# A windowed-attention and ternary-FFN layer: all masks of the scores in their second pass, one transfer that copies the high query rows, values projected sooner

## The chip, the cores and the metric

The kernel runs on one core of one Trainium2 chip. The time is device microseconds (us) of one execution. All times, in the text and in the rows, are microseconds unless ns is written. Engines are named as in the profile: PE is TensorE (PEld its weight loads), DVE is VectorE, ACT is ScalarE, POOL is GpSimd, SP is SyncE, which here only issues DMAs (SPq in the rows). PSUM is the memory that matmuls write, in eight banks.

## What is computed

The reference, cut to its core. `x` is 4 x 2048 x 256 in float32, 16 heads of 16 numbers, a causal window of 64 positions.

```python
def attn(x):                       # x already layer-normed
    q, k, v = (heads(x @ W.T) for W in (Wq, Wk, Wv))
    bias = where((j <= i) & (j > i - 64), 0.0, -inf)
    p = softmax(q @ k.T / sqrt(16) + bias)
    return merge(p @ v) @ Wo.T

def ffn(x):                        # x already layer-normed
    t = lambda W: clip(round(W / (mean(abs(W)) + 1e-5)), -1, 1)
    return relu(x @ t(W1).T + b1) @ t(W2).T + b2

x = x + attn(layernorm(x))
x = x + ffn(layernorm(x))
```

## The kernel before

**Chunks, slots, positions.** The 8192 tokens are cut into 16 chunks of 512. The program of every engine is one loop over slots n; slot n computes block n of the attention scores, 16 blocks to a chunk, so chunk c has its scores in slots 16c to 16c+15. Around the scores every engine does, in a slot, what a table of numbers at the top of the file puts there. A number in it is a slot, counted so that "position p" in this text is the slot with n mod 16 = p. Stage A of a chunk (layer norm, transposes, projections of keys K, queries Q and values V) runs one chunk ahead of its scores. Stage C (output projection `wo`, second layer norm, transposes `t`, first FFN layer `f`, second FFN layer `y`, in two halves h of 256 tokens) runs one chunk behind. So in the steady part of the program each slot mixes work of three chunks. Engines run ahead of each other as far as semaphores let them.

**Numbers are split in two.** Float32 values are carried as a high and a low float16 part. PE writes a bank, ACT copies the high part out (`c_f`, `c_t`, `a_q`, `a_k`, `a_v` on ACT), then DVE subtracts and writes the low part (same names on DVE). The bank is free when DVE is done.

**Scores of a slot** (`scores`, four head groups g, four slots each). For each of four 32-query blocks there are two matmuls of 96 columns: the first pass (m = 0) multiplies the queries in `qbd` with the keys in `ks`, the second (m = 1) adds the low part of the keys. `qbd[t]` holds high query rows on even partitions and low query rows on odd ones; t = 0 serves the groups 0 and 1, t = 1 the groups 2 and 3. In the groups 0 and 1, from chunk 1 on, the second pass reads `qm` and `kw` instead: these have the high query rows and the low keys on the even partitions and constant mask rows on the odd ones, so that the pass also adds the causal mask. In the groups 2 and 3 a matmul of its own (L1104, 256 columns) writes the mask first. The first slot of each group in each batch element (chunks 0, 4, 8, 12) has another mask matmul (L1100, 384 columns).

**After the scores**: `biggest` (DVE L827, negated maxima `negm`), `exps` (ACT L626), `turn` (DVE L844, transposes to `pt`), `low` (POOL L501 and L503, to `th` and `tl`), `values` (PE L1134, 32 or 36 matmuls, in every fourth slot: positions 0, 4, 8, 12), `o_copy` (ACT L672) and `o_add` (DVE L904). The scores of slot n wait for the exponentials of slot n-3. ACT does the exponentials of slot n-1 in slot n, DVE turns slot n-2 and POOL splits slot n-3.

**Placement.** SP copies the projected parts to their places by DMA: `place_v` (L353, 16 DMAs a chunk), `place_q` (L325, 8 DMAs for t = 1, 12 for t = 0 because the high rows go to `qm` too), `place_k` (L299 for t = 1, L302 and L305 for t = 0). SP takes them in the order of its slots and blocks on the first wait that isn't met.

**Banks.** Stages A and C share the banks 4 to 7 in turn (`_turns`): whoever comes next takes the bank that was taken four uses before, and waits until DVE has emptied it. In the steady part the first y matmul at position 2 (L1234, half 0) takes the bank of `f02`, the third quarter of the first FFN layer of half 0, which PE computes at position 0 and DVE empties at position 1 (L955).

**Where V stands**: `A_V` is (10, 13). PE projects the two halves of V (L1186, 12 matmuls of 256 columns each) at the positions 10 and 13, and DVE writes their low parts (L896) at 11 and 14.

**Start-up on POOL**: `mask_queries` fills `qm` with the mask rows at slot -16 (L397), `mask_keys` fills `kw[0]` and `kw[1]` at the slots 7 and 12 (L403), `clear_values` clears the value tiles (L414).

## Time and profile before

| | |
|---|---|
| three runs, median | 672.59 us (672.04 to 673.84) |
| profiled execution, its own time | 674.08 us |
| span of its trace | 672.3 us |
| PE busy | 645.8 us (96%), 8049 matmuls |
| DVE busy | 610.4 us (91%) |
| ACT busy | 564.0 us (84%) |
| POOL busy | 562.0 us (84%) |
| 16 DMA engines, SP's queue | 155816 packets, 41.27 MB, 29.7% |

The profiled execution is 1.5 us over the median, and 1.8 us longer than its span. Busy shares are means over stages with different limits: the first 100 us (weights, thresholds, first chunks) are not like the rest. Matmuls overlap: a matmul of 256 columns shows 273 ns in the groups, but 16 in a row take 1.75 us in the chain, 0.109 us each. The chain's starts are about 0.16 us later than the timeline's, since it goes by ends.

### The profile page before, as it was taken

Reading aid. Unit: us, or ns where it says so; the run is one execution under the profiler, and the core shown is the slowest. Engines: PE = TensorE matmul, PEld = TensorE weight load, DVE = VectorE, ACT = ScalarE, POOL = GpSimd, SP = SyncE. Lnnn points to the kernel's source line nnn. Section 1 sums busy time; section 2 is a strip of 40 time slices with the busy share of each in tenths; the row PEclk is TensorE's granted clock in tenths of the full one; section 3 lists DMA queues with packets and bytes.
Section 4 is the critical chain, followed back from the end, with each engine's and each line's share of the span. In section 5 each row is a group of like instructions: output and inputs, shape, how many; then the busy total and the mean of one; then the engine's idle time right before and its main releaser. Section 6 shows DMA issues by size and latency. Waiting matters only on the chain.

```text
span 672.3 us, 23905 instructions
## 1 busy us (share of the span) xinstructions
PE 645.8 (96%) x8049; PEld 556.4 (83%) x8049; DVE 610.4 (91%) x1388; ACT 564.0 (84%) x2483; POOL 562.0 (84%) x837
## 2 busy tenths in 40 slices
PE   7677999999999999999999999999999999998997
PEld 5465778889888888988888898888888898887886
DVE  8889799998999999998999999899999989898974
ACT  6787889888989989888998988899898989788722
POOL 8888899888889888888988888888988888798821
PEclk9899899999999999999999999999999999999999
DMA  9453444445344545444454544534454353444110
GB/s 313 104 120 73 113 87 105 98 106 123 73 130 88 134 100 117 106 96 118 83 133 97 131 106 94 127 77 119 98 135 100 65 136 67 103 87 98 37 48 32
DMA packets 187009, 70.19 MB, mean 104 GB/s; under 512 B 155268, under 2 KB 178438, under 8 KB 186888
## 3 DMA queue, kind: packets, MB, share of 16 engines
q1 hardware_dynamic: 155816, 41.27, 29.7%
q10 hardware_dynamic: 31072, 27.40, 13.4%
q8 instruction: 65, 1.06, 0.7%
q14 instruction: 56, 0.46, 0.2%
HBM read 20.35 MB, written 9.44 MB: 44 GB/s over the span
## 4 chain that ended last, share of the span: by engine, by line
PE 84%; DVE 7%; SPq 2%; ACT 2%; issue 2%; DMA 1%; ACTq 1%; DVEq 0%
PE ps L1239 16%; PE ps L1227 15%; PE ps L1134 12%; PE ps L1112 11%; PE ps L1173 11%; PE ps L1200 6%; PE ps L1186 5%; PE ps L1212 2%; PE ps L1104 2%; PE ps L1160 2%; DVE negm L827 2%; ACT p L626 1%; PE ps L1234 1%; SPq L353 1%; DVE pt L844 1%
## 5 line engine op out<-in xcount | busy, mean ns | idle before, releaser
L626 ACT ACTIVATE p<-ps,negm 128x96 f32<-128x96 f32 x1024 | 335.3, 356 | 13.6 <-DVE negm L827 12.8
L503 POOL TENSOR_TENSOR tl<-pt,th 128x384 f16<-128x384 f32 x256 | 235.0, 918 | 20.7
L626 ACT ACTIVATION_READ_ACCUMULATOR p<-ps,negm 128x1 f32 x1024 | 229.2, 224 | 0.0
L827 DVE TENSOR_REDUCE negm<-ps 128x4 f32<-128x384 f32 x256 | 137.8, 538 | 31.3 <-PE ps L1112 28.3
L501 POOL CAST th<-pt 128x384 f16<-128x384 f32 x256 | 128.8, 503 | 28.1 <-DVE pt L844 27.6
L844 DVE STREAM_TRANSPOSE pt<-p 128x384 f32<-128x384 f32 x256 | 143.6, 561 | 2.4 <-ACT p L626 2.2
L1112 PE MATMUL ps<-k,qbd 128*128 128x96 f16 x1536 | 124.8, 207 | 0.0
L1112 PEld LDWEIGHTS ps<-k,qbd 128*128 128x128 f16 x1536 | 112.4, 113 | 9.7 <-issue 0.3
L1134 PE MATMUL ps<-th,vb 128*128 128x96 f16 (+1 forms) x1120 | 99.5, 204 | 1.6 <-DVE osum L904 1.6
L1134 PE MATMUL ps<-tl,vb 128*128 128x96 f16 (+1 forms) x1120 | 99.5, 204 | 0.0
L1227 PE MATMUL ps<-xTCh,w1T 128*128 128x256 f16 x512 | 97.6, 272 | 0.0
L1134 PEld LDWEIGHTS ps<-th,vb 128*128 128x128 f16 x1120 | 95.7, 115 | 1.7 <-issue 1.7
L1134 PEld LDWEIGHTS ps<-tl,vb 128*128 128x128 f16 x1120 | 95.0, 115 | 0.0
L681 ACT ACTIVATE hTh<-ps 128x512 f16<-128x512 f32 x128 | 78.4, 614 | 14.1 <-PE ps L1227 13.6
L955 DVE SCALAR_TENSOR_TENSOR hTl<-ps,hTh 128x512 f16<-128x512 f32 x128 | 86.6, 679 | 1.7 <-ACT hTh L681 1.5
L1227 PE MATMUL ps<-xTCl,w1T 128*128 128x256 f16 x256 | 69.8, 273 | 1.0 <-DVE xTCl L948 1.0
L1227 PE MATMUL ps<-xTCl,w1L 128*128 128x256 f16 x256 | 69.8, 273 | 0.0
L1239 PE MATMUL ps<-w2T,hTl 128*128 128x256 f16 x512 | 66.7, 273 | 0.2 <-DVE hTl L955 0.2
L1239 PE MATMUL ps<-w2T,hTh 128*128 128x256 f16 x512 | 66.7, 273 | 0.0
L1112 PE MATMUL ps<-kw,qm 128*128 128x96 f16 x480 | 56.1, 208 | 0.0
L1239 PEld LDWEIGHTS ps<-w2T,hTl 128*128 128x128 f16 x512 | 49.9, 98 | 6.4 <-DVE hTl L955 0.7
L1239 PEld LDWEIGHTS ps<-w2T,hTh 128*128 128x128 f16 x512 | 49.9, 98 | 5.8 <-ACT hTh L681 0.7
(150 smaller groups left out, 1407.4 us busy)
## 6 DMA issues: line engine op xcount, KB each, us to landing
k<-kst SPq DMA_DIRECT2D x32, 288.0 KB, 3.7
rwide<-parked ACTq DMA_DIRECT2D x32, 256.0 KB
out<-x ACTq DMA_DIRECT2D x32, 256.0 KB, 2.2
qbd<-qs SPq DMA_DIRECT2D x252, 32.0 KB, 2.5
vb<-vd SPq DMA_DIRECT2D x248, 32.0 KB, 2.0
x<-in_L_attn_hidden ACTq DMA_DIRECT2D x15, 512.0 KB, 4.0
kw<-kst SPq DMA_DIRECT2D x30, 192.0 KB, 3.9
k<-kst SPq DMA_DIRECT2D x32, 144.0 KB, 3.3
```

The costliest lines, as they stand in the source:

```text
L501: e.tensor_copy(th[g % 2][:, o], pt[n % 3][:, :]).then_inc(s_hp, 1)
L503: e.tensor_tensor(tl[g % 2][:, o], pt[n % 3][:, :], th[g % 2][:, o], ALU.subtract).then_inc(s_lo, 1)
L626: ins = e.activation(p[:, 96 * u:96 * u + 96], bank[:, 96 * u:96 * u + 96], ACT.Exp, bias=m[:, u:u + 1], accum_out=r[:, u:u + 1])
L681: e.activation(hT[0][:, 2 * f:2 * f + 2, :].rearrange("p a b -> p (a b)"), c_bank(c, f"f{h}{f}")[:, :], ACT.Relu).then_inc(s_chi, 1)
L827: e.tensor_reduce(negm[n % 4][:, :], sbank[n % 3][:, 0:384].rearrange("p (a b) -> p a b", b=96), AX.X, ALU.max, negate=True).then_inc(s_mx, 1)
L844: e.transpose(pt[n % 3][:, :], pr[n % NP][:, :]).then_inc(s_tr, 1)
L955: e.scalar_tensor_tensor(out=lo, in0=c_bank(c, f"f{h}{f}")[:, :], scalar=0.0, in1=hi, op0=ALU.max, op1=ALU.subtract).then_inc(s_cdv, 1)
L1112: ins = e.matmul(bank[:, 96 * u:96 * u + 96], to[:, g % 2, blk % 4, :, blk // 4], keys, start=(g < 2 and c > 0 and not first and m == 0 an ...
L1134: ins = e.matmul(pvbank[:, 32 * i0:32 * i1], lhs, rhs, start=(k == k0 and tt is th), stop=(k == 15), skip_group_check=True)
L1173: ins = e.matmul(bank[:, :], wT[n][wp][:, k, 128 * t:128 * t + 128], xTA[xp][:, k, :], start=(m == 0), stop=(m == 5))
L1227: ins = e.matmul(bank[:, o], w, xTC[xp][:, k, :], start=(xp + k == 0), stop=(xp + k == 2))
L1239: ins = e.matmul(bank[:, o], hT[hp][:, f, t * 128:(t + 1) * 128], w2T[:, f, :], start=False, stop=(f == 7 and hp == 1))
```

## The change

1. `qm` becomes two tiles and `kw` four, and `ks[g]` holds the high keys only. In all four groups the second pass reads `qm` and `kw` from chunk 1 on, with the masks in it. The matmul L1104 stays in chunk 0 only; L1100 stays as it was.
2. `place_q` writes `qbd` only: 8 DMAs for each t. A new step `copy_q` copies the even partitions of `qbd[t]`, 64 rows of 8 KB, to `qm[t]` in one DMA. It waits for the four high DMAs of `place_q`, which have a semaphore of their own now. The scores wait for it too.
3. `place_k` issues L302-like and L305-like DMAs for all four groups: 8 a chunk instead of 6.
4. POOL fills two `qm` tiles (slots -1 and 11) and four `kw` tiles (slots 5, 8, 11, 15). The query mask is loaded to `oT[1]` instead of `pr[0]`, so the first exponentials have no wait on it any more.
5. V is projected at the positions 7 and 9. Numbers move elsewhere too: K of t = 1 from 14 to 13, `wo` from 8 and 11 to 9 and 10, the last y from 9 and 10 to 10 and 11, DMAs of K, Q, V, out and x, `O_SPLIT` from 15 to 14, `R_WIDEN` from 11 to 12, the norm's reciprocal roots from 4 to 6, and start-up slots of chunks 0 and 1.

```diff
-V_LATE = 9
-A_T, A_K, A_Q, A_V = (1, 2), (5, 14), (6, 15), (10, 13)
-A_STATS, A_RSTD, A_NORM = (-24, -14), -12, (-7, -6)
+V_LATE = (8, 11)
+A_T, A_K, A_Q, A_V = (1, 2), (5, 13), (6, 15), (7, 9)
+A_STATS, A_RSTD, A_NORM = (-24, -14), -10, (-6, -5)
...
-W_WO, K_MASK = (-6, -2), (7, 12)
-V_CLEAR = (8, 15, 19, 22, 26)
+W_WO, K_MASK, Q_MASK = (-7, -2), (5, 8, 11, 15), (-1, 11)
+V_CLEAR = (10, 15, 19, 21, 26)
...
+        def copy_q(e, c, t):
+            e.wait_ge(d_q[t], 64 * (c + 1))
+            if c == 1:
+                e.wait_ge(s_zm, t + 1)
+            to, src = (z[t][:, :, :, :, :].tensor for z in (qm, qbd))
+            e.dma_start(bass.AP(tensor=to, offset=0, ap=[[2 * 4096, 64], [1, 4096]]),
+                        bass.AP(tensor=src, offset=0, ap=[[2 * 4096, 64], [1, 4096]])).then_inc(d_qm[t], 16)
...
+                if c:
+                    e.wait_ge(d_qm[g // 2], 16 * c)
+                e.wait_ge(d_k[g], 32 * (c + 1))
                 if first:
                     e.matmul(bank[:, 0:384], identb[:, :], maskf[:, :], start=True, stop=False, skip_group_check=True)
-                elif g >= 2 or c == 0:
+                elif c == 0:
...
-                        to = qm if g < 2 and m and c else qbd[g // 2]
-                        keys = (ks[g][:, m, 32 * blk:32 * blk + 96] if g >= 2 or not m else kw[g][:, blk, :] if c
+                        to = qm[g // 2] if m and c else qbd[g // 2]
+                        keys = (ks[g][:, 32 * blk:32 * blk + 96] if not m else kw[g][:, blk, :] if c
```

How the order moves, at three places of the steady part. First DVE, from `o_add` (its first row) at position 13 on, before: the low part of the second V half is `vd`.

```order
L904 TENSOR_TENSOR osum<-ps,ohalf 64x512
L827 TENSOR_REDUCE negm<-ps 128x4
L948 TENSOR_TENSOR xTCl<-ps,xTCh 128x512
L844 STREAM_TRANSPOSE pt<-p 128x384
L827 TENSOR_REDUCE negm<-ps 128x4
L896 SCALAR_TENSOR_TENSOR vd<-ps,vd 128x2x256
L926 BN_STATS stC<-x 128x6 x2
```

DVE at the same place in the changed kernel; `kst` is the low part of the keys.

```order
L901 TENSOR_TENSOR osum<-ps,ohalf 64x512
L824 TENSOR_REDUCE negm<-ps 128x4
L945 TENSOR_TENSOR xTCl<-ps,xTCh 128x512
L841 STREAM_TRANSPOSE pt<-p 128x384
L824 TENSOR_REDUCE negm<-ps 128x4
L886 SCALAR_TENSOR_TENSOR kst<-ps,kst 128x512
L923 BN_STATS stC<-x 128x6 x2
```

The V part has left this place, and the key part has come forward by one slot; behind it the two orders are the same up to the first y.

PE from the transposes `t` of position 12 to the first matmuls of position 14, before.

```order
L1212 MATMUL ps<-identf,xnC 128x128 x4
L1104 MATMUL ps<-maskf,identb 128x4x2x32
L1112 MATMUL ps<-k,qbd 128x96 x8
L1186 MATMUL ps<-wvh,xTAh 128x256 x2
L1186 MATMUL ps<-wvl,xTAh 128x256 x2
L1186 MATMUL ps<-wvh,xTAl 128x256 x2
L1186 MATMUL ps<-wvh,xTAh 128x256 x2
L1186 MATMUL ps<-wvl,xTAh 128x256 x2
L1186 MATMUL ps<-wvh,xTAl 128x256 x2
L1104 MATMUL ps<-maskf,identb 128x4x2x32
```

PE there in the changed kernel.

```order
L1212 MATMUL ps<-identf,xnC 128x128 x4
L1112 MATMUL ps<-k,qbd 128x96
L1112 MATMUL ps<-kw,qm 128x96
...
L1173 MATMUL ps<-xTAh,wkh 128x512 x2
L1173 MATMUL ps<-xTAh,wkl 128x512 x2
L1173 MATMUL ps<-xTAl,wkh 128x512 x2
```

The two mask matmuls and the twelve V matmuls have left; the six K matmuls stand at position 13 instead of 14.

SP's DMAs over one chunk, before.

```order
L353 DMA vb<-vd 32x8x64 x16
L325 DMA qbd<-qs 16x8x128 x8
L299 DMA k<-kst 128x1x1152 x2
L325 DMA qbd<-qs 16x8x128 x4
L325 DMA qm<-qs 16x8x128 x4
L325 DMA qbd<-qs 16x8x128 x4
L302 DMA k<-kst 128x1x576
L305 DMA kw<-kst 64x16x96
```

SP's DMAs in the changed kernel, from V on.

```order
L347 DMA vb<-vd 32x8x64 x16
L299 DMA k<-kst 128x1x576
L301 DMA kw<-kst 64x16x96
L299 DMA k<-kst 128x1x576
L301 DMA kw<-kst 64x16x96
L316 DMA qbd<-qs 16x8x128 x8
L326 DMA qm<-qbd 64x4096
```

Keys of t = 1 now go ahead of the queries of t = 1, and the copy to `qm` is behind both. For t = 0 keys, queries and copy now all stand ahead of V.

## Rows read from the trace of the kernel before

**Rows 1.** Page, part 1: busy us (share of the span) and instructions, the line of all engines.
```profile
PE 645.8 (96%) x8049; PEld 556.4 (83%) x8049; DVE 610.4 (91%) x1388; ACT 564.0 (84%) x2483; POOL 562.0 (84%) x837
```
**Rows 2.** Windows: us, busy of PE, PEld, DVE, ACT, POOL (instructions), PE clock, DMA, GB/s.
```profile
25.00:50.00 25.00, 17.99 (x214) 14.26 (x212) 22.48 (x51) 21.13 (x104) 22.42 (x33) 0.86 0.48 110
75.00:100.00 25.00, 22.45 (x305) 18.72 (x303) 22.96 (x54) 22.77 (x107) 23.27 (x35) 1.00 0.40 92
425.00:450.00 25.00, 25.00 (x340) 22.31 (x338) 23.45 (x56) 22.14 (x102) 21.96 (x35) 1.00 0.41 91
```
**Rows 3.** Chain of work around one chunk: start, us, engine, line and count.
```profile
416.22 1.45 PE ps L1134 x36
...
436.12 1.44 PE ps L1134 x36
...
438.04 0.11 PE ps L1104
...
438.49 1.31 PE ps L1186 x12
...
450.12 0.12 PE ps L1234
...
454.96 1.45 PE ps L1134 x36
```
**Rows 4.** Groups of PE's instructions by line: busy us, mean ns, idle before.
```profile
L1104 PE MATMUL ps<-maskf,identb 128*128 128x256 bf16 x126 | 34.6, 275 | 3.7 <-DMA k<-kst 2.0 <-ACT p L626 1.7
```
**Rows 5.** Timeline of ACT, DVE and PE between the values of position 12 and y.
```profile
437.60 0.59 ACT L672 ACTIVATE ohalf<-ps 64x512 f32<-64x512 f32 x1 [0.48 <-PE ps L1134]
438.22 0.69 DVE L904 TENSOR_TENSOR osum<-ps,ohalf 64x512 f32<-64x512 f32 x1
440.95 0.67 DVE L896 SCALAR_TENSOR_TENSOR vd<-ps,vd 128x512 f16<-128x512 f32 x1
441.55 0.73 DVE L926 BATCH_NORM_STATS2 stC<-x 128x6 f32<-128x256 f32 x2
449.22 0.68 DVE L955 SCALAR_TENSOR_TENSOR hTl<-ps,hTh 128x512 f16<-128x512 f32 x1
449.96 0.28 PE L1234 MATMUL ps<-bp,ones 128*128 128x256 f16 x1
```
**Rows 6.** Timeline of PE, first y of the last chunk's slots, where stage A is absent.
```profile
605.47 0.82 PE L1239 MATMUL ps<-w2T,hTl 128*128 128x256 f16 x6
606.45 0.39 PE L1239 MATMUL ps<-w2T,hTl 128*128 128x256 f16 x2 [0.17 <-DVE hTl L955]
```
**Rows 7.** Timeline of SP and PE, last chunk: DMA issues, and scores that wait for keys.
```profile
613.83 1.22 SPq L299 DMA_DIRECT2D k<-kst  x2
617.35 0.27 PE L1104 MATMUL ps<-maskf,identb 128*128 128x256 bf16 x1 [2.02 <-DMA k<-kst]
```
**Rows 8.** Timeline of SP in one chunk: start and length of issues.
```profile
441.66 11.47 SPq L353 DMA_DIRECT2D vb<-vd  x16
414.48 5.90 SPq L325 DMA_DIRECT2D qbd<-qs  x8
434.84 1.42 SPq L305 DMA_DIRECT2D kw<-kst  x1
```
**Rows 9.** DMA issues: KB each, median us from issue to landing.
```profile
k<-kst SPq DMA_DIRECT2D x32, 288.0 KB, 3.7
x<-in_L_attn_hidden ACTq DMA_DIRECT2D x15, 512.0 KB, 4.0
kw<-kst SPq DMA_DIRECT2D x30, 192.0 KB, 3.9
```
**Rows 10.** Timeline of POOL in the start-up: start, us, idle before in brackets.
```profile
8.43 1.90 POOL L397 COPY qm<-p 128x2048 f32<-128x2048 f32 x1 [0.95 <-DVE xnA L850]
35.11 1.47 POOL L403 COPY kw<-oTl 128x1536 f16<-128x1536 f16 x1
72.15 0.96 POOL L414 MEMSET vb<- 128x1024 f32 x1 [2.05 <-DVE w2T L820]
```

More of the change, by code:

```diff
@@ L65, in v_at @@
     c = stage_a(n, A_V[t])
-    return c if t else 1 if n == V_LATE else None if c == 1 else c
+    return 0 if n == F_V[t] - 16 else c if c and c > 1 else 1 if n == V_LATE[t] else None
 def spread(n, pos, soonest):
@@ L131, in _turns @@
     late = {("C", NCH - 1, "wo1"): E_WO[1] + 0.5, ("C", NCH - 1, "t1"): E_T[1] - 0.5}
-    order = [(V_LATE if (stage, c, name) == ("A", 1, 4) else 16 * (c + (1 if stage == "C" else -1)) + late.get((stage, c, name), p), stage == "A", i, stage, c, name)
+    order = [(V_LATE[name - 4] if (stage, c) == ("A", 1) and name in (4, 5) else F_V[name - 4] - 16 if (stage, c) == ("A", 0) and name in (4, 5) else 16 * (c + (1 if stage == "C" else -1)) + late.get((stage, c, name), p), stage == "A", i, stage, c, name)
              for c in range(NCH) for i, ((stage, name), p) in enumerate(pos.items())]
@@ L200, in build @@
         qbd = [sb(f"qbd{t}", [128, 2, 4, 128, 4], f16) for t in range(2)]
-        qm = sb("qm", [128, 2, 4, 128, 4], f16)
-        ks = [sb(f"k{g}", [128, 1 + g // 2, 64 + CH], f16) for g in range(4)]
-        kw = [sb(f"kw{g}", [128, 16, 96], f16) for g in range(2)]
+        qm = [sb(f"qm{t}", [128, 2, 4, 128, 4], f16) for t in range(2)]
+        ks = [sb(f"k{g}", [128, 64 + CH], f16) for g in range(4)]
+        kw = [sb(f"kw{g}", [128, 16, 96], f16) for g in range(4)]
         vd = sb("vd", [128, 4, 2, 4, 16, 4], f16)
@@ L232, in build @@
         d_w = {n: sem(f"d_w{n}") for n in "qkvo12"}
-        d_q = [sem(f"d_q{t}") for t in range(2)]
+        d_q, d_ql, d_qm = ([sem(f"{n}{t}") for t in range(2)] for n in ("d_q", "d_ql", "d_qm"))
         d_k = [sem(f"d_k{g}") for g in range(4)]
@@ L265, in build @@
         n1, n2 = n1.rearrange("p (a b) -> p a b", b=256), n2.rearrange("p (a b) -> p a b", b=1024)
-        smask, kmask = pr[0][:, 0:256].bitcast(f16), oT[1][:, 1, 0:96]
+        smask, kmask = oT[1][:, 0, :], oT[1][:, 1, 0:96]
         bt = (hT[0][:, :, :].rearrange("p a b -> p (a b)").bitcast(f32), hT[1][:, 0:2, :].rearrange("p a b -> p (a b)").bitcast(f32))
         below = hT[1][:, 4:8, :].rearrange("p a b -> p (a b)").bitcast(f32)
-        first_kl = [kw[g][:, :, :].rearrange("p a b -> p (a b)")[:, 0:64 + CH] for g in range(2)]
+        first_kl = [kw[g][:, :, :].rearrange("p a b -> p (a b)")[:, 0:64 + CH] for g in range(4)]
         def by_four(bank):
@@ L293, in place_k @@
                     e.wait_ge(s_sc, 16 * (c - 1) + 4 * g + 4)
-                if c == 1 and t == 0:
+                if c == 1:
                     e.wait_ge(s_kw, g + 1)
@@ L376, in _ @@
                     if c is not None:
-                        place_q(e, c, t, (0, 1, 2) if c or t else (0,))
+                        place_q(e, c, t, (0, 1) if c or t else (0,))
                         if c + t == 0:
                             place_k(e, 0, 0, (1,))
+                    c = stage_a(n, Q_COPY[t])
+                    if c is not None and c >= 1:
+                        copy_q(e, c, t)
                 c = spread(n, V_DMA, 17)
@@ L527, in _ @@
                     mask_keys(K_MASK.index(n))
+                if n in Q_MASK:
+                    mask_queries(Q_MASK.index(n))
                 for h in range(2):
@@ L705, in _ @@
                 if n == A_Q[0] + 2 - 16:
-                    place_q(e, 0, 0, (2,))
+                    place_q(e, 0, 0, (1,))
                 if n in X_LATE:
@@ L1108, in scores @@
                     for m in range(2):
-                        to = qm if g < 2 and m and c else qbd[g // 2]
-                        keys = (ks[g][:, m, 32 * blk:32 * blk + 96] if g >= 2 or not m else kw[g][:, blk, :] if c
+                        to = qm[g // 2] if m and c else qbd[g // 2]
+                        keys = (ks[g][:, 32 * blk:32 * blk + 96] if not m else kw[g][:, blk, :] if c
                                 else first_kl[g][:, 32 * blk:32 * blk + 96])
                         ins = e.matmul(bank[:, 96 * u:96 * u + 96], to[:, g % 2, blk % 4, :, blk // 4], keys,
-                                       start=(g < 2 and c > 0 and not first and m == 0 and u == 0),
+                                       start=(c > 0 and not first and m == 0 and u == 0),
                                        stop=(m == 1 and u == 3), skip_group_check=True)
```

69 lines of the change are left out of this document (28 added, 41 removed).

## The prediction, made before the changed kernel ran

> **What bounds the kernel now.** I read the shares first: PE is busy for 96% of the span, DVE for 91%, ACT and POOL for 84% [rows 1]. A mean doesn't tell which stage is bound by what, so the windows come next: in a window of the steady part PE is busy for 25.00 of 25.00 us, DVE for 23.45 [rows 2]. In the start-up PE is busy for 17.99 us between 25 and 50 and for 22.45 us between 75 and 100 [rows 2], so others set the pace there. From about 92 to 600 us PE is the bound, without a gap. A chunk takes 454.96 - 416.22 = 38.74 us [rows 3]; DVE's share of that is 23.45 / 25 x 38.74 = 36.3 us. So a chunk can lose at most 2.4 us before DVE is full, and DVE must have no gap anywhere for that.
>
> **The masks go.** L1104 runs 126 times [rows 4]; 12 are in chunk 0 and stay, 114 go, 8 in each later chunk less 6 for the first slots of the chunks 4, 8 and 12, which have the other mask. The groups show 275 ns for one, which is its latency; the chain gives 0.11 us from one to the next [rows 3], and the y matmuls of the same 256 columns 0.109. So 114 x 0.109 = 12.4 us of PE work. 8 of them stand in chunk 1, in a stretch in which PE has gaps anyway [rows 2], so I count 106 x 0.109 = **11.6 us**. The second pass costs PE the same with either operand.
>
> **What V's move does to DVE.** This is the step on which the prediction rests. Between the values of position 12 and the y of position 2 DVE has hardly a gap: values end, ACT copies their half at 437.60, DVE adds at 438.22, and from there on DVE works through to the low part of `f02`, which starts at 449.22 and takes 0.68, so ends at 449.90. PE starts y at 449.96 [rows 5], in the bank that this very instruction empties. So PE has 0.06 us to spare there, in a kernel that seems to be bound by PE alone. From the last value to y PE takes 450.12 - 437.56 = 12.56 us by the chain (437.56 is 436.12 + 1.44) [rows 3]. The other way, ACT's copy, DVE's work and two hand-overs, takes about 12.5.
>
> The change shortens the two by different amounts. PE loses the 12 V matmuls, 1.31 us [rows 3], and the mask matmuls of the positions 13, 14 and 15, 0.33: it needs 12.56 - 1.64 = 10.92 us. DVE loses only the low part of V, 441.55 - 440.95 = 0.60 us [rows 5]: about 11.85. K of t = 1 moves inside the stretch and changes neither sum. So PE comes to y 0.93 us early and waits for the bank: **a new stall of 0.9 us in every chunk**, where 0.87 us of masks is saved. Both kernels have y's of half 0 in 14 chunks before the scores end: 14 x 0.9 = 12.6 us.
>
> Could DVE be faster in this stretch? Its anchor is the addition of the values (`o_add`), and that can't start before PE has written them; what DVE does earlier (one V part less at position 11, one at 8 and one at 10 more) is over by then, since there PE's slots keep V's 1.31 us. Position 12 itself gets shorter on PE and DVE alike. Bounds of the stall: 0.4 if DVE had 0.5 us of hidden waits inside (the profile shows under 0.1), 1.3 if ACT's or POOL's part of the chain slips by 0.4: POOL's second norm of the half 1 tiles comes after both multiplications and splits, since `O_SPLIT` moved up. 0.9 stands since each term has its row.
>
> The trace holds a trial of this. In the last chunk's slots stage A is absent, so PE lacks 0.44 us of transposes ahead of y while DVE's part of this is the same. There the last two low matmuls of y start at 606.45, though six of 0.109 from 605.47 end at 606.12 [rows 6]: PE stands for 0.33 us, for DVE. 0.44 us taken from PE gave back 0.11.
>
> **The last chunk's keys.** At the scores of slot 248 PE waits 2.02 us for the keys of t = 1, which SP issues last, at 613.83 [rows 7]. In the changed kernel V is issued some 5 us sooner and the keys stand right behind it; last is the copy to `qm`. V's 16 DMAs take 11.5 us, four of keys at most 1.4 each, 8 of queries 5.9 [rows 8], the copy 0.6 and a landing like that of 512 KB, 4.0 [rows 9]. Counted from the V part at position 10, that is 2.4 + 11.5 + 3.4 + 5.9 + 0.6 + 4.0 = 27.8 us; in the steady part the scores of group 2 come 34 us after it, in the last chunk, with its short slots, about 29. So the wait goes: **-2.0 us** (bounds -2.0 and 0).
>
> **DMA traffic.** Per chunk two copies of 512 KB and two more `kw` placements of 192 KB come, four query DMAs go. A copy is priced between a 288 KB placement, 3.7, and the 512 KB load, 4.0 [rows 9]; to 8 us if an 8 KB row doesn't spread. All of it is hidden by the 6 us above, and by over 10 us for t = 0, which is ahead of V. The `kw` placement moves 192 KB in pieces of 192 B in 3.9 us, the keys' 288 KB in 3.7 [rows 9]: 1.6 times longer per byte.
> The Trainium skill ("DMA: Bandwidth & Descriptors", Specifications) asks for pieces of at least 512 B for full rate, which speaks against two more such placements. The trace agrees as to the rate; by that rule too the sum stays while the cover holds, and it is the third rival if it doesn't.
>
> **Start-up.** POOL gets two mask copies of 1.47 us and one of 1.90 more [rows 10] between 28 and 60 us; the first of 1.90 moves from 8.43 to the time before the first split, and V's early projection lets POOL place it 1 us sooner, which covers half. POOL has 25 - 22.42 = 2.6 us of gaps between 25 and 50 [rows 2], and DVE's turns have three tiles of lead, so I expect nothing there. Later, the clearing at slot 22 already waits 2.05 us for a weight [rows 10]; at slot 21 it waits for the same weight with one split fewer done, so POOL is 1.4 us later at about 73 us and works without a gap until 100. By then DVE, not POOL, leads most of the time: **+0.5 us** (bounds -1 and +4.5).
>
> **Sum.** -11.6 + 12.6 - 2.0 + 0.5 = -0.5 us. Against the profiled execution's 674.08 that is 673.6; it lies 1.5 over the median, so 672.59 - 0.5 = **672.1 us**. The masks' time is given back at y.
>
> **Rivals.**
> - *The cover holds.* If y doesn't wait, since DVE's work has more give than I read (its instruction starts are 0.44 to 0.60 us apart, no one is proven tight), all of the masks count: 672.6 - 11.6 - 2.0 + 0.5 = 659.5. For it: 25 of 25 us of PE, DVE at 94% only. Against it: the 0.06 us and the stall in the last chunk. Half a stall gives 665.8. Chance 0.22.
> - *Slower: POOL in the start-up.* The 4.8 us of mask copies and the 1.4 us at the clearing put POOL behind by more than the lead of three `pt` tiles. DVE's turn of a slot waits for POOL's split of three slots before; once POOL is later than that lead, about 4 us, DVE stops, with it the exponentials and the scores. If all but 1.2 of the 6.2 us come through, the sum has 5.0 instead of 0.5: 676.6. For it: POOL is 90% busy from 25 to 50. Against it: its gaps, and the long lead. Chance 0.20.
> - *Slower: the copies come late.* The copy can't start before the high rows have landed, and for t = 1 it is the last in SP's queue. From a landing of some 10 us on (cover 6, plus 4) each further us costs 15 us over the chunks; 1 us more is 687. Nothing in the rows is that slow. Chance 0.05.
> - The forecast's mechanism, with the stall between 0.6 and 1.1: 0.53; its own range is 668 to 675.
>
> **How the numbers follow.** A measurement of this kernel can tell 0.3%, 2.0 us, from no change: faster is below 670.6, slower above 674.6. Of the forecast's 0.53 I put 0.11 below, 0.38 within and 0.04 above. The first rival is all faster, the two others are slower but for 0.03. Faster 0.33, same 0.41, slower 0.26. The range of 8 in 10 runs from 662 (half of the first rival) to 679 (all of the second).
>
> **What would show it.** Right, if in the profile after PE has gaps of about 0.9 us at the first bias matmul of y (L1234's successor) at position 2, with the low part of `f02` ending just ahead, if the chunk still takes 38.8 us and if PE's busy time falls while its share of the span falls by two points. The group of mask matmuls must count 12. The wait for keys near the end must be gone. Wrong, if a chunk takes 37.9 us; wrong too if PE waits at scores (for DMAs or exponentials) rather than at y.

## The result, and the profile after

The changed kernel takes 674.19 us (median of 17 runs, 673.85 to 675.48), the kernel before 672.23 us in the same comparison (17 runs, 670.63 to 675.86). The ratio is 1.0027, with an interval of 1.0016 to 1.0037: 2.0 us slower, where 0.5 us faster was forecast. The two profiled executions, though, took 674.16 and 674.08 us, a difference of 0.1. So the first question is which of the two differences is the change's. The changed kernel again on another chip (e1) took 674.41 us against 672.63; that ratio's interval just reaches no change. Executions more than 1.5% above the fastest of their kernel (744.87 of the kernel before, 2295.24 in e1, 718.93 in e3) are left out of all ratios.

The page of the changed kernel, parts 1, 3 and 6 in extracts (busy us, share, instructions; queue, packets, MB, share; issues, KB, us to landing), answers to [rows 1, 9]:

```profile
PE 637.5 (95%) x7935; PEld 544.5 (81%) x7935; DVE 611.5 (91%) x1388; ACT 560.6 (83%) x2483; POOL 567.5 (84%) x840
...
q1 hardware_dynamic: 181064, 56.50, 38.5%
...
qm<-qbd SPq DMA_DIRECT2D x30, 512.0 KB, 4.2
kw<-kst SPq DMA_DIRECT2D x60, 192.0 KB, 3.9
k<-kst SPq DMA_DIRECT2D x64, 144.0 KB, 3.2
```

PE has 114 matmuls less, as counted. Its busy time fell by 8.3 us and the span didn't. PE's waits at y, from the waits (us in total, times, longest):

```profile
PE ps L1234 <- DVE hTl L952: 7.6, 12, 0.7
```
The chain of work at the place of [rows 3] and [rows 5] (start, us, what):

```profile
438.04 1.46 PE ps L1134 x36
439.51 0.60 ACT ohalf L669
...
443.54 0.67 DVE stC L923 x2
...
449.23 0.69 DVE osum L901
449.95 0.47 DVE negm L824
450.43 0.69 DVE hTl L952
451.45 1.75 PE ps L1239 x16
```

From the end of the values of position 12 to y the chain runs over ACT and DVE now, not over PE. The last thing ahead of y is DVE's low part of `f02`, L952. The y itself in the timeline, with its gap in brackets, for two chunks in a row:

```profile
412.37 0.28 PE L1234 MATMUL ps<-bp,ones 128*128 128x256 f16 x1 [0.67 <-DVE hTl L952]
...
450.30 0.21 PE L1112 MATMUL ps<-kw,qm 128*128 128x96 f16 x1
451.17 0.28 PE L1234 MATMUL ps<-bp,ones 128*128 128x256 f16 x1 [0.67 <-DVE hTl L952]
```

The last matmul ahead of y in the kernel before, where y started at 449.96 [rows 5]:

```profile
449.91 0.21 PE L1112 MATMUL ps<-kw,qm 128*128 128x96 f16 x1
```

451.17 - 412.37 = 38.80 us for a chunk, against 38.74 before [rows 3]. The bracket counts PE's idle time from the end of the last matmul, and so it understates the wait. That matmul shows 0.21 us, but in the kernel before y starts 0.05 us after its start, since matmuls overlap. After the change y starts 451.17 - 450.30 = 0.87 us after it. So PE stands about 0.83 us. The window of just this chunk, from y to y (columns as in [rows 2]):

```profile
412.37:451.17 38.80, 38.13 (x493) 33.11 (x493) 36.54 (x85) 34.26 (x155) 33.71 (x51) 1.00 0.56 135
```
And the window of one chunk of the kernel before, from y to y:

```profile
411.22:449.96 38.74, 38.74 (x505) 33.96 (x502) 36.48 (x85) 34.51 (x156) 33.65 (x51) 1.00 0.46 108
```

PE's busy time falls by 0.61 us and its idle time is 0.67 us, but both leave out what hides behind the length of overlapping matmuls. By the starts, the eight mask matmuls were 8 x 0.109 = 0.87 us of work. PE stands 0.83 us of that at y and 0.09 us at the first f of position 14, whose low matmul now starts 0.30 us after the high pair (441.77 to 442.07) and not 0.22 us (440.09 to 440.31 before). That adds up: 38.74 - 0.87 + 0.83 + 0.09 = 38.79 us. DVE's work is the same. At the end of the program the key wait of 2.02 us [rows 7] is gone, and the wait inside the last such y has grown from 0.17 [rows 6] to 0.99 us:

```profile
607.97 0.39 PE L1239 MATMUL ps<-w2T,hTl 128*128 128x256 f16 x2 [0.99 <-DVE hTl L952]
```

### The profile page after: what moved, and what is told of

Same layout as the page of the kernel before. It is cut to its first block, busy times and chain, and to the rows that moved or that the text cites. A ratio compares the mean times of both kernels' runs of the same rounds, so it can differ in the third digit from the quotient of the medians.

```text
span 672.4 us, 23939 instructions
## 1 busy us (share of the span) xinstructions
PE 637.5 (95%) x7935; PEld 544.5 (81%) x7935; DVE 611.5 (91%) x1388; ACT 560.6 (83%) x2483; POOL 567.5 (84%) x840
## 4 chain that ended last, share of the span: by engine, by line
PE 52%; DVE 23%; POOL 13%; issue 7%; ACT 1%; DVEq 0%; POOLq 0%
PE ps L1239 14%; PE ps L1227 8%; PE ps L1134 7%; PE ps L1112 6%; DVE negm L824 6%; PE ps L1173 5%; POOL tl L500 5%; DVE hTl L952 5%; PE ps L1200 4%; PE ps L1186 4%; DVE pt L841 3%; POOL th L498 2%; DVE stC L923 2%; DVE osum L901 2%; DVE kst L886 1%
## 5 line engine op out<-in xcount | busy, mean ns | idle before, releaser
L622 ACT ACTIVATION_READ_ACCUMULATOR p<-ps,negm 128x1 f32 x1024 | 236.7, 232 | 0.0
L1112 PE MATMUL ps<-k,qbd 128*128 128x96 f16 x1024 | 119.7, 208 | 0.6 <-ACT p L622 0.5
L1112 PE MATMUL ps<-kw,qm 128*128 128x96 f16 x960 | 111.9, 208 | 0.0
L1112 PEld LDWEIGHTS ps<-k,qbd 128*128 128x128 f16 x1024 | 101.6, 114 | 10.8 <-ACT p L622 1.5
L1112 PEld LDWEIGHTS ps<-kw,qm 128*128 128x128 f16 x960 | 89.4, 114 | 6.9 <-issue 0.8
L952 DVE SCALAR_TENSOR_TENSOR hTl<-ps,hTh 128x512 f16<-128x512 f32 x128 | 86.5, 679 | 1.7 <-ACT hTh L678 1.5
L669 ACT ACTIVATE ohalf<-ps 64x512 f32<-64x512 f32 x64 | 38.7, 605 | 26.5 <-PE ps L1134 25.8
```

Of the source, the lines that this page charges most:

```text
L622: ins = e.activation(p[:, 96 * u:96 * u + 96], bank[:, 96 * u:96 * u + 96], ACT.Exp, bias=m[:, u:u + 1], accum_out=r[:, u:u + 1])
L669: e.activation(ohalf[:, :], pvbank[0:64, :], ACT.Copy).then_inc(s_oc, 1)
L952: e.scalar_tensor_tensor(out=lo, in0=c_bank(c, f"f{h}{f}")[:, :], scalar=0.0, in1=hi, op0=ALU.max, op1=ALU.subtract).then_inc(s_cdv, 1)
L1112: ins = e.matmul(bank[:, 96 * u:96 * u + 96], to[:, g % 2, blk % 4, :, blk // 4], keys, start=(c > 0 and not first and m == 0 and u == 0), ...
```

## The experiments

Fifteen kernels besides the two, in five groups. The medians, with the kernel before on the same chip beside each, and the ratio to it:

| run | edit | median us | before | ratio, interval |
|---|---|---|---|---|
| e1 | changed kernel again | 674.41 | 672.63 | 1.0019, 0.9999 to 1.0039 |
| e2 | statistics at 12 | 676.01 | 672.63 | 1.0039, 1.0020 to 1.0058 |
| e3 | V half 1 at 12 | 711.65 | 672.63 | 1.0523, 1.0476 to 1.0571 |
| e4 | before, V half 1 at 11 | 688.90 | 672.63 | 1.0228, 1.0192 to 1.0264 |
| e5 | t1 at position 2 | 716.47 | 673.33 | 1.0655, 1.0633 to 1.0676 |
| e6 | masks by SP's DMAs | 680.53 | 673.33 | 1.0110, 1.0090 to 1.0130 |
| e8 | before, last keys first | 676.93 | 673.33 | 1.0060, 1.0037 to 1.0084 |
| e9 | masks by ACT's DMAs | 672.62 | 673.38 | 0.9996, 0.9982 to 1.0010 |
| e10 | short statistics | 668.08 | 673.38 | 0.9933, 0.9914 to 0.9951 |
| e11 | before, short statistics | 673.10 | 673.38 | 1.0003, 0.9982 to 1.0023 |
| e13 | before, POOL load | 674.31 | 673.16 | 1.0015, 0.9997 to 1.0033 |
| e14 | wo1 at 13 | 678.89 | 673.16 | 1.0088, 1.0066 to 1.0109 |
| e16 | bn_stats at 11 | 668.13 | 673.01 | 0.9920, 0.9897 to 0.9943 |
| e17 | e16 and e9 | 666.68 | 673.01 | 0.9894, 0.9868 to 0.9919 |

Further there are e7 (e5 and e6 together, 723.06, ratio 1.0737, interval 1.0712 to 1.0761), e15 (e14 and e9 together, 676.75, ratio 1.0058, interval 1.0036 to 1.0079) and e12, one execution of the kernel before for its profile (672.51). For e7 663 us was expected and for e15 664.5; both hung on e5 and e14, which failed.

A ratio compares kernels on one chip. Differences between two of the experiments, below, are mostly between chips: the kernel before alone has medians of 672.23 to 673.38 in the six comparisons.

### Is the stall at y what holds the pace? One cut that moves nothing

```diff
-                    e.bn_stats(stC[:, t, :], xs[c % NX][:, 2 * u + t, :]).then_inc(s_stC, 1)
+                    e.bn_stats(stC[:, t, :], xs[c % NX][:, 2 * u + t, 0:32 if u else D]).then_inc(s_stC, 1)
```

> The changed kernel with part of the computation left out: the second norm's statistics of half 1 are taken over 32 of 256 columns. DVE's two instructions for them at position 14, inside its unbroken run from the values' addition to the low part of f02, get some 0.6 us shorter together. Order, banks, waits and PE's work are as they were, so nothing can move elsewhere as in the runs that moved a step. Theory 1 (PE stands at y because DVE's run is longer than PE's way): the stall at y shrinks by 0.6 us, to 0.1 at most, the chunk falls from 38.80 to 38.2 and the kernel by 13 to 14 times 0.6, to 666. Theory 2 (y waits for something else): 674.

> The kernel before with the same part left out (statistics of half 1 over 32 of 256 columns). There PE has its V part and mask matmuls in this stretch and 0.06 us to spare, by the prediction's reading. Theory 1: PE is the bound of the steady part, so DVE's 0.6 us a chunk is worth nothing, 672.5, with the chunk at 38.7. If it gets faster by several us, DVE led in the kernel before too and the reading of before was wrong. A further profile of its start-up shows where its first y comes (101.3, 98.5 and 99.9 us in the three profiles so far).

In e10 the two instructions take 0.27 us together instead of 0.73, and y's gap falls by just that, from 0.67 to 0.20. Timeline of DVE in e10:

```profile
439.88 0.27 DVE L923 BATCH_NORM_STATS2 stC<-x 128x6 f32<-128x32 f32 x2
```
Timeline of PE in e10:

```profile
408.78 0.28 PE L1234 MATMUL ps<-bp,ones 128*128 128x256 f16 x1 [0.20 <-DVE hTl L952]
...
447.12 0.28 PE L1234 MATMUL ps<-bp,ones 128*128 128x256 f16 x1 [0.20 <-DVE hTl L952]
```

A chunk takes 447.12 - 408.78 = 38.34 us, 0.46 less, and the kernel 674.41 - 668.08 = 6.3 us less (two chips; the ratios to the kernel before, 0.9933 and 1.0027, give the same), which is 14 times 0.45. Expected were 0.6 and 8 us, since I took the cut for larger than it is. In the kernel before the same cut gives nothing (673.10 against 673.38). So the same DVE work is free before the change and on the path after it. This shows theory 1.

### Moving whole steps: each time a new wait

The edits of e2, e14, e3 and e5, in this order. In e2 the last chunk keeps 14; e4 is the kernel before with `A_V` at (10, 11).

```diff
-C_WO, C_STATS, C_RSTD = (9, 10), (10, 14), (12, 16)
+C_WO, C_STATS, C_RSTD = (9, 10), (10, 12), (12, 16)
+C_WO, C_STATS, C_RSTD = (9, 13), (10, 14), (12, 16)
-A_T, A_K, A_Q, A_V = (1, 2), (5, 13), (6, 15), (7, 9)
+A_T, A_K, A_Q, A_V = (1, 2), (5, 13), (6, 15), (7, 12)
-C_T, C_F, C_Y = (12, 17), (14, 20), (18, 26)
+C_T, C_F, C_Y = (12, 18), (14, 20), (18, 26)
```

> The changed kernel again, beside the three edits of this call and the kernel before on one chip. If the predicted stall holds the pace, a chunk of the steady part takes 38.8 us again and PE stands some 0.67 us of it at the first y. Against the kernel before: the two profiles taken so far differ by 0.1 us, the medians of 17 runs by 1.96 us (674.19 against 672.23). If the medians are right, this gives a ratio of 1.002 to 1.004; if the profiled pair is right, 1.000.

> The changed kernel with the second norm statistics of stage C at position 12 instead of 14 (except in the last chunk). They take DVE 1.19 us (443.46 to 444.65 in the profile after), between the values of position 12 and the y of position 2. PE's work is as before the edit. Theory 1 (PE waits at y since DVE comes late to the bank of f02): DVE comes 1.19 us sooner, the stall of 0.67 us a chunk goes, the chunk takes 38.1 us, and over 13 to 14 chunks the kernel falls by 9 us, to 665. Theory 2 (something else than DVE's work in this stretch sets y, such as the exponentials on ACT or a DMA): 674, with the stall as it was. Theory 3 (the statistics at position 12 hold up the values' addition behind them, which is the stretch's start): DVE gains nothing, 674, and the addition of position 13 comes about 1 us later.

> The changed kernel with the second half of V projected at position 12 instead of 9. That puts 1.31 us of PE and 0.60 us of DVE back between the values of position 12 and y, and moves them out of another place, so neither engine's sum changes. Theory 1 (stall by DVE's lateness relative to PE in this stretch): PE needs 0.71 us more than DVE's part grows, the stall of 0.67 us is used up, the chunk takes 38.1 us and the kernel 665. Theory 2 (something else sets y): 674. Theory 3 (the V placement, which starts some 7 us later, makes the keys, queries or the copy for the groups 2 and 3 late): PE waits at the scores of position 8 for a DMA, 15 times some 1 to 3 us, and the kernel gets slower, 680 or more.

> The kernel before, masks and all, with the second half of V at position 11 instead of 13. No work is added or taken away; 1.31 us of PE and 0.60 us of DVE leave the stretch between the values of position 12 and y. Theory 1: PE had 0.06 us to spare there, so it now stands 0.65 us a chunk at y (less if the stall measures smaller than its sum, as 0.67 instead of 0.93 did in the changed kernel: then 0.4), and the kernel gets 5.5 to 9 us slower, 678 to 682. Theory 2 (PE's work alone is the bound): no change, 672.5.

> The changed kernel with the second transposes of stage C (t, half 1) at position 2 behind the first y instead of position 1. No work is added, removed or made longer, but the banks' turn moves: the first y of half 0 now takes the bank of the second query part of position 15, which DVE has emptied some 2.2 us before y, instead of the bank of f02. Theory 1 (PE waits at y for the bank of f02): the wait of 0.67 us at L1234 goes. What is left is the data of f03: its low part ends about 1.3 us after y's present start, and y's low matmuls for it come 1.6 us after y's start, so 0.3 us at most of a new wait at L1239. A chunk falls from 38.80 to 38.1 or 38.4, the kernel from 674.3 to 665 to 668. Theory 2 (DVE's work as a whole sets the pace, whatever the bank): the wait moves to L1239 or to the second f in full and the time stays 674.

> The changed kernel with the second output projection (wo of half 1) at position 13 instead of 10. It puts 1.31 us of PE and 0.60 us of DVE (its residual) into the stretch from the scores of position 13 to y, behind the point from which DVE works without a gap, and takes them from position 10. PE's and DVE's sums are as they were. Theory 1 (PE stands at y by the difference of the two engines' work in the stretch): PE's way grows by 0.7 us more than DVE's, the wait of 0.67 us at y goes nearly, the chunk takes 38.1 to 38.2 and the kernel 666. Theory 2 (DVE's whole work of the chunk is the bound, 36.5 of 38.8 us): no change, 674. Theory 3 (statistics, reciprocal roots and the norm behind wo come too late for the transposes of position 1): a new wait there, and 674 or more.

PE's waits in e2 (us in total, times, longest):

```profile
PE ps L1227 <- DVE xTCl L945: 13.2, 15, 2.4
```
In e3:

```profile
PE ps L1112 <- DMA qm<-qbd: 20.4, 9, 5.3
PE ps L1234 <- DVE hTl L952: 10.6, 13, 1.0
```
In e4:

```profile
PE ps L1227 <- DVE xTCl L948: 17.8, 15, 1.4
```
In e5:

```profile
PE ps L1227 <- DVE x L916: 29.0, 14, 2.2
PE ps L1239 <- DVE hTl L952: 14.8, 14, 2.0
```

- **e2**: the wait at y is gone, 0.88 us a chunk stand at the first f of position 14 instead. The 1.19 us ahead of the addition were more than DVE's idle time there (0.56 and 0.43 us), so the addition and the low part of t came later. Theory 3 held.
- **e4**: the wait is 1.19 us a chunk, not 0.65, and it stands at f, not at y. Theory 2 is out; of theory 1 the slowdown came, but larger and at another place. In the kernel before, V at position 13 covers the way t, ACT, DVE, f. I had not seen this use of it. The change keeps the cover, by K at 13. That V's move is harmless there rests on K's, which I had costed at nothing without naming the work that it covers.
- **e3**: two findings. The placement of V 3 slots later makes the copies to `qm` late: 20.4 us in 9 waits and 6.3 more at the first slots of batch elements. The cover of the copies is thus below the 7 us or so that V moved, as the prediction had it (6 us). And the stall at y grew, 10.6 / 13 = 0.82 us, though PE got 1.31 us more.
- **e14** shows why. PE got its 1.31 us behind the scores of position 13, and the stall grew again, to 0.95. DVE's timeline there:

```profile
407.69 0.56 DVE L824 TENSOR_REDUCE negm<-ps 128x4 f32<-128x384 f32 x1 [0.51 <-PE ps L1112]
408.16 0.68 DVE L916 SCALAR_TENSOR_TENSOR x<-ps,x 128x512 f32<-128x512 f32 x1
```

DVE now waits for the scores of position 14, which stand behind `wo` and K on PE. Its unbroken run starts there instead of at the addition, with the residual in it. Work given to PE ahead of scores delays DVE as well, so it covers nothing. "PE's way minus DVE's way" holds only between the last point at which DVE waits for PE and y. The two runs refute the remedy, not the reading of the stall. Besides, e14's first y comes at 105.01, so some 3 us of the 4.5 that it is slower than e1 lie in the start-up.
- **e5** tested the bank alone. The first y has no wait at L1234 any more, so it was the bank of `f02`. But the second f of half 1 took the bank of that y, one slot after it, and waits 2.1 us for its residual (x, L916), and y's low part waits for f03. A chunk takes about 42 us. Here the wait for one bank was exchanged for a wait for another.

### Moving only as much as fits

```diff
+            def c_sums(c, u):
+                e.wait_ge(s_cdv, USE[c, f"wo{u}"] + 1)
+                for t in range(2):
+                    e.bn_stats(stC[:, t, :], xs[c % NX][:, 2 * u + t, :]).then_inc(s_stC, 1)
...
+                    c = stage_c(n, 11)
+                    if u and c is not None and c < NCH - 1:
+                        c_sums(c, 1)
```

> The changed kernel with the two bn_stats of half 1 (0.73 us on DVE together) at position 11, behind the residual of wo that they read, and only their aggregation (0.46 us) at position 14. Nothing is left out. DVE has two waits, of 0.56 and 0.43 us, between position 11 and the values' addition at 13, so the moved work fits ahead of the stretch, unlike the 1.19 us that the run with all of it at position 12 moved there. Theory 1 (the stall at y is DVE's unbroken run from the addition to the low part of f02): the run gets 0.73 us shorter, the wait of 0.67 us at y goes, and no new one comes at the first f; the chunk takes 38.1 to 38.3 us and the kernel 665 to 667. Theory 2 (any us moved ahead comes back through the addition): a new wait at L1227 or L1112 of some 0.5 us a chunk and 674.

> The edit of e16 together with that of e9 (mask rows by DMAs that ACT issues, no mask copies on POOL). If the two causes are separate, start-up and steady part, the gains add: 665 to 667 less 1.8, so 663.5 to 665, against 673.2 for the kernel before. If e16 gives nothing, 672.6.

Timeline of DVE ahead of the addition in e16:

```profile
432.57 0.75 DVE L922 BATCH_NORM_STATS2 stC<-x 128x6 f32<-128x256 f32 x2
433.24 0.56 DVE L841 STREAM_TRANSPOSE pt<-p 128x384 f32<-128x384 f32 x1
433.73 0.52 DVE L824 TENSOR_REDUCE negm<-ps 128x4 f32<-128x384 f32 x1
...
435.64 0.69 DVE L901 TENSOR_TENSOR osum<-ps,ohalf 64x512 f32<-64x512 f32 x1 [0.32 <-ACT ohalf L669]
```
The first y of two chunks in PE's timeline of e16, with the matmul ahead of the second:

```profile
407.86 0.28 PE L1241 MATMUL ps<-bp,ones 128*128 128x256 f16 x1
...
445.80 0.21 PE L1119 MATMUL ps<-kw,qm 128*128 128x96 f16 x1
446.13 0.28 PE L1241 MATMUL ps<-bp,ones 128*128 128x256 f16 x1
```
The low part of `f02` in DVE's timeline of e16:

```profile
445.39 0.68 DVE L956 SCALAR_TENSOR_TENSOR hTl<-ps,hTh 128x512 f16<-128x512 f32 x1
```
The window between the two y:

```profile
407.86:446.13 38.27, 38.14 (x492) 33.14 (x493) 36.62 (x85) 34.32 (x155) 33.76 (x51) 1.00 0.59 137
```

The moved 0.75 us fill the former wait of 0.56 us, and the addition still waits for ACT, 0.32 instead of 0.43: it comes no later relative to PE. No new wait comes at f, whose low matmul starts 0.30 us after the high pair as in the changed kernel.

The wait at y shrinks, but it isn't gone, as theory 1 had it. The row of y has no bracket, since only 0.12 us lie between it and the end of the matmul ahead. By the starts it comes 0.33 us after that matmul instead of 0.04, and 0.06 us after the low part of `f02` ends (445.39 + 0.68 = 446.07). So PE still stands 0.29 us in such a chunk, for the same bank. DVE's way from the addition to the start of that low part is 0.54 us shorter (9.75 against 10.29 us), not 0.73. The chunk adds up again: 38.74 - 0.87 + 0.29 + 0.09 = 38.25 us, and 38.27 is measured. With no wait at all it would be 37.87 us, an estimate from these rows.

Against the changed kernel's 674.4 (e1) e16 has 6.3 us less; 665 to 667 was expected and 668.1 came. e17 adds the start-up's part and takes 666.7 us, ratio 0.9894 to the kernel before; 663.5 to 665 was expected. Of the kernels here it is the fastest, and faster than both.

### The start-up

> The kernel before again, for a second profile of the very program. The profiled execution of before took 674.1, its median is 672.2 to 673.3. If the profiled one was slow in its start-up, this one has its first y at 98.5 to 100.5 us instead of 101.3, with the same 38.74 us a chunk behind it; the four profiles of the changed kernel and its variants have it at 101.8 to 102.1.

> The kernel before with three copies on POOL that nobody needs, at the slots 8, 11 and 15, of the shapes of the changed kernel's additional mask copies (about 1.5, 1.9 and 1.5 us, 4.8 together). Nothing else changes, so its steady part is that of before (38.74 us a chunk). Theory 1 (POOL's added work in the start-up is the 2 us by which the changed kernel measures slower): the first y moves from 98.6 to 100 or later in every run, and the median rises by 1.5 to 3 us over that of before, to 674.5 to 676. Theory 2 (POOL has room; what else was moved in the start-up, V's early projection or the order, costs the time): median unchanged, first y at 98.6 to 101.3 as before.

> The changed kernel with the mask rows of the query and key tiles written by six DMAs from DRAM (odd partitions only) instead of six copies on POOL. POOL loses 4 x 1.47 + 2 x 1.90 = 9.7 us of work before 60 us; the steady part is untouched. Theory 1 (POOL paces the start-up of the changed kernel, as the slower rival of the prediction said, and this is why it measures 2 us over the kernel before although the two profiles agree): the first y comes 3 us or more before the 101.8 us of the changed kernel, and the kernel takes 671 or less. Theory 2 (the thresholds and the folding of the FFN weights on DVE, ACT and PE pace it): first y at 101.8, 674.

> The changed kernel without the six mask copies on POOL; the mask rows come by six DMAs from DRAM again, but ACT issues them (0.4 to 1.2 us each, as its other issues in the start-up), so that SP's queue is that of the changed kernel. In the run with SP issuing them the last copy of the second chunk came at 76.6 instead of 69.7 us and PE stood 7.8 us for it, which hid what POOL's relief gives. Theory 1 (POOL paces the start-up of the changed kernel): first y well before 101.9 us, by 2 us or more, and 672 or less. Theory 2 (other engines pace it): first y at 101.9, 674.3; somewhat more if ACT's six issues are on the path.

e13 adds three copies to a tile of its own at the slots 8, 15 (the first form) and 11 (the second):

```diff
+                if n in (8, 15):
+                    e.tensor_copy(load[:, 0:3, :].rearrange("p a b -> p (a b)").bitcast(f16).rearrange("p (a b) -> p a b", b=96),
+                                  kmask.unsqueeze(1).to_broadcast([128, 16, 96]))
+                if n == 11:
+                    e.tensor_copy(load[:, :, :], identf[:, 0:1].unsqueeze(1).to_broadcast([128, 8, 256]))
```

e9 removes `mask_keys` and `mask_queries` from POOL, and ACT issues in their place (in e6 SP does, for the queries at the slots 2 and 4, for the keys inside `place_k` of chunk 1):

```diff
+                if n in (1, 6):
+                    e.dma_start(bass.AP(tensor=qm[n // 6][:, :, :, :, :].tensor, offset=4096, ap=[[2 * 4096, 64], [1, 4096]]),
+                                bass.AP(tensor=smask_d.tensor, offset=512, ap=[[2 * 512, 64], [0, 8], [1, 512]])).then_inc(d_s[n // 6], 16)
+                if n in (5, 9, 13, 17):
+                    g = n // 4 - 1
+                    e.wait_ge(s_sc, 4 * g + 4)
+                    e.dma_start(bass.AP(tensor=kw[g][:, :, :].tensor, offset=1536, ap=[[2 * 1536, 64], [1, 1536]]),
+                                bass.AP(tensor=kmask_d.tensor, offset=96, ap=[[2 * 96, 64], [0, 16], [1, 96]])).then_inc(d_km[g], 16)
```

The very first y in PE's timeline of before:

```profile
101.28 0.28 PE L1234 MATMUL ps<-bp,ones 128*128 128x256 f16 x1
```
Of the same kernel in e12:

```profile
98.64 0.28 PE L1234 MATMUL ps<-bp,ones 128*128 128x256 f16 x1
```
Of the changed kernel:

```profile
101.78 0.28 PE L1234 MATMUL ps<-bp,ones 128*128 128x256 f16 x1
```
Of e16:

```profile
101.64 0.28 PE L1241 MATMUL ps<-bp,ones 128*128 128x256 f16 x1
```
Of e17:

```profile
99.98 0.28 PE L1233 MATMUL ps<-bp,ones 128*128 128x256 f16 x1
```

The profiled execution of before was late in the start-up, by 2.64 us against e12. e11 (98.75) and e8 (99.87) have the same start-up program, but for e11's shorter statistics. Five profiles that keep the changed kernel's start-up (after, e1, e2, e3, e10) have 101.67 to 102.13. So the start-up of before comes out short or long, and that of after was long in all five. This fits the spread of the 17 runs, 5.2 us for before and 1.6 for after, of which most have no profile.

**Where the changed kernel loses it.** ACT's first exponential of slot 20 starts at 70.05 in e12 and at 71.37 in the changed kernel, that of slot 28 at 87.25 and 90.10. So 1.3 us are lost up to slot 20 and 1.5 more between the slots 20 and 28; the last 0.3 are mostly the first y's own wait for `f02`.

**The mask copies on POOL are a part of it, the one up to slot 20.** e17 removes all six (9.7 us, also the three that the kernel before has) from e16: on the same chip its median is 1.45 us less, the two ranges don't meet, and its first y comes 1.66 us sooner. Its slot 20 comes at 69.76, no later than in e12. e9 removes them from the changed kernel: 1.8 us faster than e1, though on another chip, with its first y at 101.11 in an execution of 673.52, one of its slower ones. Its theory 1 had wanted 2 us at the first y. What the three added copies alone cost is less sure. e13 puts as much, 4.8 us, on POOL in the kernel before: 1.15 us slower by the medians, but the ratio's interval, 0.9997 to 1.0033, takes in no change. Its first y at 101.12 says nothing, since before's own goes from 98.64 to 101.28. And its runs still spread over 4.9 us, so these copies alone don't take the short start-up away.

**The part between the slots 20 and 28 is another matter.** e17 has it too (69.76 to 88.52 us), so the mask copies don't make it. PE's timelines there show two waits for POOL, for a low part of the probabilities and for the second norm. In the changed kernel:

```profile
85.30 0.21 PE L1134 MATMUL ps<-th,vb 128*128 128x32 f16 x1 [0.78 <-POOL tl L500]
...
88.92 0.66 PE L1212 MATMUL ps<-identf,xnC 128*128 128x128 f32 x4 [1.98 <-POOL xnC L488]
```
In e17:

```profile
83.72 0.21 PE L1133 MATMUL ps<-th,vb 128*128 128x32 f16 x1 [0.72 <-POOL tl L485]
...
87.34 0.66 PE L1211 MATMUL ps<-identf,xnC 128*128 128x128 f32 x4 [1.98 <-POOL xnC L473]
```

e12 has 1.40 us at the norm and no such wait for the low part. Which of the other moves (V sooner, the split, the norms, the clears) makes POOL late there is open: no run took one of them back.

**e6** had the same relief of POOL and was 6.1 us slower than e1. SP issued the six DMAs itself, and the copy to `qm` for the groups 2 and 3 of chunk 1 was issued at 76.58. SP's timeline:

```profile
71.00 5.53 SPq L318 DMA_DIRECT2D qbd<-qs  x8
76.58 0.60 SPq L326 DMA_DIRECT2D qm<-qbd  x1
```
PE's timeline:

```profile
82.64 0.24 PE L1102 MATMUL ps<-k,qbd 128*128 128x96 f16 x1 [7.80 <-issue]
```

In the changed kernel that copy is issued at 71.62. The profile names no releaser for the 7.80 us; that it is this copy, 5 us later than before, is the likely reading. The first y comes at 108.42.

### The last keys

```diff
                     c = spread(n, K_DMA[t], A_K[t] + 2)
+                    if t and (c == NCH - 1 or stage_a(n, 17) == NCH - 1):
+                        c = stage_a(n, 17)
```

> The kernel before with one step of one chunk moved: for the last chunk SP issues the keys of t = 1 ahead of V instead of behind V and the queries. Nothing else changes. The wait of 2.02 us for these keys at slot 248 must go. Theory 1 (the prediction's term of -2.0): the end comes 2 us sooner, 670.5. Theory 2 (behind slot 248 the pace is set by the chain values, addition, normalisation, splits on DVE and POOL, which didn't wait for these keys): the scores come 2 us sooner and the last y doesn't, 672.5. Besides, its start-up is that of the kernel before, to the instruction: if the first y comes at 98.5 as in the run with V at 11 and not at 101.3 as in the profile of before, the start-up of before varies by 3 us from run to run.

Neither came. The keys' own condition (the scores of position 15 done) held SP, and V and the queries behind it, until 598.59; the queries were issued last, at 612.15. The wait at slot 248 is 4.69 us instead of 2.02 to 2.72, and from the y of position 2 to the last y it takes 669.70 - 603.13 = 66.57 us instead of 62.39 (e12: 63.11). So a wait there can reach the end, and more than fully; V and the queries were later too, and their part isn't separated. That the wait would give its 2 us back when removed was not measured alone. SP's timeline in e8:

```profile
598.59 1.18 SPq L299 DMA_DIRECT2D k<-kst  x2
599.87 12.17 SPq L353 DMA_DIRECT2D vb<-vd  x16
612.15 5.10 SPq L325 DMA_DIRECT2D qbd<-qs  x8
```

## Why the prediction was wrong, by its own steps

Differences after - before, from y to y of half 0, by the two profiles of the kernel before. The forecast's terms stand in the stretch that they belong to: of the 14 stalls of 0.9 one lies before the first y's start and one in the last stretch, and so do 16 of the 106 masks of 0.109.

| stretch | forecast | against the profile before | against e12 |
|---|---|---|---|
| to the first y | +1.4 (0.5 and a stall) | +0.50 | +3.14 |
| 12 chunks from there, to y at 566.18, 563.93 and 567.64 | +1.0 (-9.8 + 10.8) | +0.96 | +0.57 |
| from there to the last y, at 666.87, 665.33 and 666.97 | -2.8 (-1.7 - 2.0 + 0.9) | -1.36 | -2.07 |
| sum | -0.5 (rounded) | +0.10 | +1.64 |

- **The step that failed is the start-up, "+0.5", together with the last step, "it lies 1.5 over the median, so 672.59 - 0.5".** Both take the start-up of the one profile for that of the kernel before. The 1.5 us by which it lay over the median are more than covered by its start-up, 2.64 us longer than e12's, whose execution (672.51) is near the median. I carried them over to the changed kernel as if they were a constant. The changed kernel was never seen with a faster start-up: its profiled execution, 674.16, is at its median, 674.19. Against a typical execution the start-up term is +3.1, not +0.5, and the medians' difference, 1.96 us, is close to that against e12, 1.64.
- **Start-up, in parts.** 1.3 us arise up to slot 20, and POOL's mask copies can explain them, since without all six 1.4 to 1.8 us less are measured (e17, e9): the mechanism of the second rival, at less than its price. 1.5 us arise between the slots 20 and 28, with PE waiting for POOL; their cause is open.
- **The agreement of the two profiled executions is partly luck.** -0.5 was forecast and +0.1 came, but the start was 0.9 less than its terms and the end 1.4 more.
- **Masks, 0.87 us a chunk, and the new stall of 0.93.** Right, mechanism and sizes: by the starts 0.87 us of mask work went, and PE stands 0.83 us at y and 0.09 at f. The net, +0.06, is the measured 38.80 - 38.74. That the stall takes the masks' gain is shown by e10 and e11, and that it was PE against DVE and not PE alone by e16, where 6.3 us come out although 0.29 us of the stall are left.
- **DVE's way between the values and y, "loses only the low part of V", 11.85 us.** Right: in the timeline PE starts on what follows the values at 439.32 and on y at 451.17, 11.85 us later. What I had not seen is that V at 13, and now K, covers the way from t to f (e4).
- **Key wait, -2.0.** It is gone, but the last stretch is only 1.4 to 2.1 us shorter. If its 16 masks (1.7 us) and the grown wait inside its y (0.8 us) count in full, 0.5 to 1.2 us are left for the keys. No run separates the three.
- **Copies hidden.** Right: no wait for `qm` in the profile after, landing 4.2 us in the median. The cover is small: V 3 slots later uses it up (e3). The prediction also read 192 KB in 3.9 us against 288 KB in 3.7 as a lower rate of the short pieces and as agreement with the rule on them. The rows don't bear that out: 144 KB in rows of 1152 B took 3.2 us, which is more per byte than the 192 B pieces needed.

## What to carry to other kernels

When one engine's work is cut, look for the next unbroken run of another engine to the same meeting point, and cut there too: here 0.73 us moved into an existing gap of DVE turned a change worth nothing into 6 us. Move only as much as the gap holds, and ask what a moved step covered where it stood. Measure a wait from start to start and not by the idle time shown: where matmuls overlap, 0.29 us of waiting showed no bracket at all. And before a difference of profiles is added to a median, take a second profile of the same kernel: a spread of the runs (5 us here) suggests that one stretch has more than one length, and a change can leave only the long one.

## What the runs showed of the hardware

The length of before's start-up goes with the granted clock of TensorE. Windows of the profile before:

```profile
25.00:35.00 10.00, 6.58 (x48) 4.51 (x46) 7.90 (x23) 8.33 (x44) 9.30 (x16) 0.67 0.40 88
60.00:75.00 15.00, 10.73 (x99) 8.07 (x100) 12.68 (x24) 10.39 (x47) 11.81 (x18) 0.77 0.43 92
```
Windows of e12:

```profile
25.00:35.00 10.00, 7.01 (x45) 4.49 (x46) 7.97 (x24) 7.93 (x41) 9.36 (x16) 0.66 0.37 81
60.00:75.00 15.00, 11.48 (x128) 8.04 (x129) 13.43 (x26) 12.19 (x54) 12.58 (x18) 0.89 0.44 96
```

From 25 to 35 us both executions had the lower level (1.2 GHz, 0.50 in the rows) for equally long. From 60 to 75 us the profile before had it for twice as long (0.77 against 0.89). PE had been busy for 1.88 us of the 5 ahead of 65 us there, for 2.54 in e12. e4, e8 and e11 also have 0.89 from 60 to 75 us, with first y at 98.53, 99.87 and 98.75; e13 has 0.77 and 101.12. Over whole executions the same shows: of the executions of the kernel before beside the experiments, the 11 with a mean granted clock of 0.995 have a median of 671.77 us and the 7 with 0.987 one of 676.15. The changed kernel depends on it less: two runs with 0.994 and 0.995 took 674.16 and 674.02 us, three with 0.987 took 674.93 to 675.48. From 25 to 35 us it had 0.83 in one profile and 0.66 in the other (e1), and its first y came at 101.78 and 101.97. Whether the clock makes the start-up long, or a late start-up lets the clock fall, is open: no run changed the clock alone.

A copy of 512 KB inside SBUF, 64 partitions of 8 KB, landed in 3.2 to 7.0 us, 4.2 in the median, about as 512 KB from DRAM did before (4.0, [rows 9]). And bn_stats over 32 instead of 256 columns took 0.27 instead of 0.73 us for two, so by an estimate from these two some 0.1 us of each doesn't depend on the columns.
